# Two sets of GELU buffers in the low-rank FFN of a two-block transformer layer

## The reference

```
x = x + attn_a(layernorm(x))   # causal attention with low-rank q and kv, rope, 16 heads, scores clipped to +-80
x = x + ffn(layernorm(x))
x = x + attn_b(layernorm(x))   # causal attention in a window of 256, 16 heads
x = x + ffn(layernorm(x))

def ffn(x):                    # U1 1024x256, V1 256x4096, U2 4096x256, V2 256x1024
    P = x @ U1
    H = gelu(P @ V1 + b1)      # the tanh form of gelu
    Q = H @ U2
    return Q @ V2 + b2
```

## Time and profile before

| | |
|---|---|
| median of 3 runs | 16249.39 us (16242.38 to 16249.87) |
| the profiled execution, its own time | 16244.88 us |
| its span, slowest core (core 1) | 16243.3 us |
| spans of the 8 cores | 16207.3 to 16243.3 us |
| mean granted TensorE clock of the cores | 0.536 to 0.540 of full speed |
| busy on core 1 | PE 5935.0, PE weight loads 4271.9, DVE 5274.7, ACT 4021.9, POOL 118.0 us |

### The profile page before, as it was taken

How to read it: one execution, slowest core, us unless ns; L and a number is a source line. 1 busy time by engine, 2 the same in 40 slices (tenths; PEclk the granted TensorE clock), 3 DMA queues, 4 the chain that set the end, 5 groups by cost and what they waited for, 6 DMA issues and landing times.

```text
span 16243.3 us, 153437 instructions; the slowest of 8 cores (16207.3 to 16243.3 us)
## 1 busy us (share of the span) xinstructions
PE 5935.0 (37%) x54352; PEld 4271.9 (26%) x54352; DVE 5274.7 (32%) x7648; ACT 4021.9 (25%) x9384; POOL 118.0 (1%) x228
## 2 busy tenths in 40 slices
PE   2333322333333344344443333333333333333333
PEld 1111112222233233333343222222222222222222
DVE  0111134444444444444444322232233222232233
ACT  2222222222222222222232222222222222222222
POOL 0000000000000000000000000000000000000000
PEclk6555555555555555555555555555555555555555
DMA  1111011111122122222232200000000000000000
GB/s 64 37 37 37 31 32 33 35 38 45 51 58 63 48 62 70 54 79 60 72 81 54 83 19 6 6 6 6 6 6 6 3 6 6 6 6 6 6 6 4
DMA packets 197816, 540.34 MB, mean 33 GB/s; under 512 B 33876, under 2 KB 34261, under 8 KB 192600
## 3 DMA queue, kind: packets, MB, share of 16 engines
q1 hardware_dynamic: 177112, 463.40, 10.7%
q0 software_dynamic: 19968, 67.12, 1.0%
HBM read 463.29 MB, written 67.11 MB: 33 GB/s over the span
## 4 chain that ended last, share of the span: by engine, by line
DVE 29%; PE 29%; ACT 25%; issue 10%; DMA 5%; ACTq 1%; SPq 1%; DVEq 1%; POOL 0%; POOLq 0%
DVE bufA L342 11%; PE pf L649 7%; ACT ptb L557 7%; DVE pbig L551 4%; ACT hb L322 4%; PE pbig L542 3%; PE pbig L350 2%; PE acc L579 2%; DVE htb L344 2%; DVE bufA L333 2%; ACT bufA L326 2%; ACT bufB L336 2%; DMA arena<-vS 2%; PE pbf L284 2%; ACT xnT L288 2%
## 5 line engine op out<-in xcount | busy, mean ns | idle before, releaser
L551 DVE TENSOR_SCALAR pbig<-pbig 128x1024 f32<-128x1024 f32 x1056 | 1251.6, 1227 | 2016.6 <-PE pbig L542 2016.6
L342 DVE RECIPROCAL bufA<-bufB 128x512 f32<-128x512 f32 x512 | 1716.7, 3353 | 53.6 <-DVE bufB L339 0.9
L312 PE MATMUL pbig<-ptf,W_v 128*128 128x128 bf16 x4096 | 518.0, 306 | 3303.7 <-ACT bufB L336 3264.8
L557 ACT ACTIVATE ptb<-pbig 128x1024 bf16<-128x1024 f32 x1056 | 1081.1, 1024 | 2383.2 <-DVE pbig L551 2331.6
L579 PE MATMUL acc<-arena,ptb 128*128 128x64 bf16 x8448 | 815.0, 215 | 1336.3 <-ACT ptb L557 1109.6
L312 PEld LDWEIGHTS pbig<-ptf,W_v 128*128 128x128 bf16 x4096 | 396.4, 138 | 3425.3 <-issue 3425.3
L649 PE MATMUL pf<-xnT,arena 128*64 128x128 bf16 x8192 | 1055.2, 309 | 615.1 <-ACT qTs L656 309.3
L542 PE MATMUL pbig<-arena 96*128 96x128 bf16 x8448 | 986.0, 311 | 446.7 <-DMA arena<-vS 440.1
L322 ACT ACTIVATE hb<-pbig,sb_b1r 128x128 f32<-128x128 f32 x2048 | 584.4, 368 | 2272.5 <-DVE htb L344 2188.8
L579 PEld LDWEIGHTS acc<-arena,ptb 128*128 128x128 bf16 x8448 | 705.0, 126 | 1504.2 <-issue 1504.2
L649 PEld LDWEIGHTS pf<-xnT,arena 128*64 128x64 bf16 x8192 | 838.5, 166 | 830.2 <-issue 830.2
(11 more groups left out here) (108 smaller groups left out, 7154.8 us busy)
## 6 DMA issues: line engine op xcount, KB each, us to landing
arena<-kcS SPq DMA_DIRECT2D x528, 256.0 KB, 3.5
arena<-vS SPq DMA_DIRECT2D x528, 256.0 KB, 3.5
arena<-krS SPq DMA_DIRECT2D x528, 128.0 KB, 3.8
xa<-x SPq DMA_DIRECT2D x64, 512.0 KB, 5.3
x2S<-x2sb POOLq DMA_DIRECT2D x32, 512.0 KB, 4.6
xa<-x2S SPq DMA_DIRECT2D x32, 512.0 KB, 3.8
out<-x2sb POOLq DMA_DIRECT2D x32, 512.0 KB, 4.5
rc<-ropec SPq DMA_DIRECT2D x32, 256.0 KB, 4.9
```

The costliest lines, as they stand in the source:

```text
L312: emit("tensor", lambda e, j=j, l=l, pb=pb, jj=jj: e.matmul(pbig[:, pb + jj * 128:pb + (jj + 1) * 128], wb["v1"][:, l * 4096 + j * 128:l * ...
L342: emit("vector", lambda e: e.reciprocal(out=sg[:], in_=dd[:]), incs=[("v", 1)])
L551: emit("vector", lambda e, h0=h0: e.tensor_scalar(out=pbig[:, h0 * 128:(h0 + 8) * 128], in0=pbig[:, h0 * 128:(h0 + 8) * 128], scalar1=80.0 ...
L557: emit("scalar", lambda e, kb=kb, h0=h0: e.activation(out=ptb[kb][:, h0 * 128:(h0 + 8) * 128], in_=pbig[:, h0 * 128:(h0 + 8) * 128], func= ...
```

## The change

The work tiles of the GELU chain now exist twice. Even groups use `hb0`, `bufA`, `bufB`; odd groups use `hb1`, `bufC`, `bufD`. The rope tables `rc` and `rs` lose their own memory and lie in `bufC` and `bufD`. The waits of the loop name a count in place of "everything so far": TensorE waits, ahead of L312 of group g, for the bias additions of group g-2 (which read the same PSUM region), and ScalarE waits, ahead of L322, for L344 of group g-2 (the last reader of the same work tiles). Ahead of the square ScalarE is given the same wait once more. Group 0 has in addition the wait of TensorE for all of ScalarE's work. The order of the instructions in every queue stays as it was, and so do their number, shapes and types. No DMA is added, removed or moved.

```diff
-        rc = [T("rc0", [128, 512])]
-        rs = [T("rs0", [128, 512])]
...
-        hb = T("hb", [128, 512])
+        hbb = [T("hb0", [128, 512]), T("hb1", [128, 512])]
         bufA = T("bufA", [128, 512])
         bufB = T("bufB", [128, 512])
+        bufC = T("bufC", [128, 512])
+        bufD = T("bufD", [128, 512])
...
+        rc = [bufC]
+        rs = [bufD]
...
+                idmark = {0: 0, 1: 0}
+                htmark = {0: 0, 1: 0}
                 for g in range(8):
                     pb = 1024 + (g % 2) * 512
-                    wait("tensor", "s")
+                    hb = hbb[g % 2]
+                    A_ = bufA if g % 2 == 0 else bufC
+                    B_ = bufB if g % 2 == 0 else bufD
+                    wait("tensor", "s", idmark[g % 2])
+                    if g == 0:
+                        wait("tensor", "s")
...
                     wait("scalar", "t")
-                    wait("scalar", "v")
+                    wait("scalar", "v", htmark[g % 2])
...
+                    idmark[g % 2] = cnt["s"]
                     wait("scalar", "s")
-                    emit("scalar", lambda e: e.activation(out=sq[:], in_=hb[:], func=AF.Square),
+                    wait("scalar", "v", htmark[g % 2])
+                    emit("scalar", lambda e, hb=hb, A_=A_: e.activation(out=A_[:], in_=hb[:], func=AF.Square),
                          incs=[("s", 1)])
...
-                    emit("vector", lambda e, g=g: e.tensor_tensor(out=htb[:, g * 512:(g + 1) * 512],
-                                                                  in0=hb[:], in1=sg[:], op=ALU.mult),
+                    emit("vector", lambda e, g=g, hb=hb, A_=A_: e.tensor_tensor(out=htb[:, g * 512:(g + 1) * 512],
+                                                                                in0=hb[:], in1=A_[:], op=ALU.mult),
                          incs=[("v", 1)])
+                    htmark[g % 2] = cnt["v"]
```

More of the change, by code:

```diff
@@ L318, in ffn @@
                     wait("scalar", "t")
-                    wait("scalar", "v")
+                    wait("scalar", "v", htmark[g % 2])
                     for jj in range(4):
                         j = g * 4 + jj
-                        emit("scalar", lambda e, j=j, jj=jj, pb=pb: e.activation(
+                        emit("scalar", lambda e, j=j, jj=jj, pb=pb, hb=hb: e.activation(
                             out=hb[:, jj * 128:(jj + 1) * 128], in_=pbig[:, pb + jj * 128:pb + (jj + 1) * 128],
@@ L324, in ffn @@
                             func=AF.Identity, bias=b1r[:, j:j + 1]), incs=[("s", 1)])
+                    idmark[g % 2] = cnt["s"]
                     wait("scalar", "s")
-                    emit("scalar", lambda e: e.activation(out=sq[:], in_=hb[:], func=AF.Square),
+                    wait("scalar", "v", htmark[g % 2])
+                    emit("scalar", lambda e, hb=hb, A_=A_: e.activation(out=A_[:], in_=hb[:], func=AF.Square),
                          incs=[("s", 1)])
                     wait("vector", "s")
-                    emit("vector", lambda e: e.tensor_scalar(out=u0[:], in0=sq[:], scalar1=GC2,
-                                                             scalar2=GC1, op0=ALU.mult, op1=ALU.add),
+                    emit("vector", lambda e, A_=A_, B_=B_: e.tensor_scalar(out=B_[:], in0=A_[:], scalar1=GC2,
+                                                                           scalar2=GC1, op0=ALU.mult, op1=ALU.add),
@@ L331, in ffn @@
                          incs=[("v", 1)])
                     wait("vector", "v")
-                    emit("vector", lambda e: e.tensor_tensor(out=uu[:], in0=u0[:], in1=hb[:], op=ALU.mult),
+                    emit("vector", lambda e, hb=hb, A_=A_, B_=B_: e.tensor_tensor(out=A_[:], in0=B_[:], in1=hb[:], op=ALU.mult),
                          incs=[("v", 1)])
                     wait("scalar", "v")
-                    emit("scalar", lambda e: e.activation(out=ee[:], in_=uu[:], func=AF.Exp, scale=-2.0),
+                    emit("scalar", lambda e, A_=A_, B_=B_: e.activation(out=B_[:], in_=A_[:], func=AF.Exp, scale=-2.0),
@@ L337, in ffn @@
                          incs=[("s", 1)])
                     wait("vector", "s")
-                    emit("vector", lambda e: e.tensor_scalar_add(out=dd[:], in0=ee[:], scalar1=1.0),
+                    emit("vector", lambda e, B_=B_: e.tensor_scalar_add(out=B_[:], in0=B_[:], scalar1=1.0),
                          incs=[("v", 1)])
                     wait("vector", "v")
-                    emit("vector", lambda e: e.reciprocal(out=sg[:], in_=dd[:]), incs=[("v", 1)])
+                    emit("vector", lambda e, A_=A_, B_=B_: e.reciprocal(out=A_[:], in_=B_[:]), incs=[("v", 1)])
```

## The result

The changed kernel takes 15199.56 us (median of 8 runs, 15193.92 to 15204.0), beside 16245.64 us for the kernel before in the same comparison: a ratio of 0.9356 with a 95% interval of 0.9346 to 0.9366. It is faster by 1046 us. The prediction was 15290 us with a range of 15230 to 15400. Those 90 us are what the experiments are about.

A forecast was written before the change was run, and what follows sets the result against it. The prediction took a relay between engines, not a full engine, to bound the kernel. 448 x 2.14 = 959 us off 16244.88 gave 15286, plus 4.5 for the median, so 15290 us; other terms were 0; range 15230 to 15400.

The forecast's parts named there:

- The relay and its passages: GELU loop, L344 to L329 of the next group: 2.75 us becomes 0.61, saving 2.14 us in each of 448 passages.
- rival 1: L344 to L329: VectorE needs 0.80 us instead of 0.61, as for dependent pairs; 15376 us, chance 0.08.
- rival 2: L322 and L326 under L342: ScalarE and VectorE don't run together in SBUF; saving 0.37 us a passage, 16084 us, chance 0.04.
- rival 4: Loop waits: a count still covers L344 of group g-1 or another wait blocks; old relay, 16249 us, chance 0.02.
- rival 5: Reciprocal L342: stretched by ScalarE's traffic, making the kernel slower; 16791 us if it doubled, chance 0.02.
- TensorE's wait: Ahead of L312: its matmuls move forward by more than a group, but nothing waits for them; 0 us.
- the tiles of the rope tables: `rc` and `rs` in `bufC` and `bufD`: used in phase 1 alone, with a barrier between; 0 us.
- the second wait: Ahead of the square L326: same count as ahead of L322, hence already met; 0 us.
- the instant of the rise: TensorE's clock rising within L350 behind the loop: put near 0, far ends 178 us lost or 205 us gained.
- no distance moves: Outside the loop: a sign expected in the profile after, that no distance there changes.
- rival 3: Clock behind the loop, at L350, moves: 15468 or 15085 us at the ends, chance 0.06 for both sides together.
- L350 clearly away from 6.4 us: L350's 64 matmuls: a total clearly different from 6.4 us would be the sign of rival 3.

The follow-up runs named there:

- the two kernels with Q in the loop: Kernel before and changed kernel, each with the 8 matmuls of Q that need group g run inside the loop: 15976.93 and 14961.81 us.

## Why the prediction was right, and where it was wrong

**The relay and its passages: right.** 448 passages at 2.14 us were to give 959 us; the loop gave 968. The start of L341 0.61 us behind L356, the group of 6.64 us (6.65 expected), ScalarE's idle time of 4.2 us ahead of the exponential (about 4.0 expected) and the 766 us left ahead of L329 (some 780 expected) came as written, but for L332, which starts 0.09 us before the exponential's end and not behind it. Of the 9 us more, about half is the passage shown, 8.79 - 6.64 = 2.15 us and not 2.14; the other half lies in passages that had run longer than the one shown: before, a loop took 4335.2 / 64 = 67.74 us, 0.17 more than 6.04 + 7 x 8.79; after, 52.61, 0.10 more than 6.03 + 7 x 6.64.

**Rivals 1, 2, 4 and 5: fell.** The trace gives 0.61 us and not 0.80, the reciprocal 3352 to 3354 ns with ScalarE at work under it, and L332 is not released by the group before any more. With the Trainium skill's statement (SBUF — State Buffer, "Who interferes with whom") that ScalarE and VectorE have their own ports the trace agrees: 3353 ns alone, 3353 and 3352 ns together.

**TensorE's wait, the tiles of the rope tables, the second wait: right at 0.** The run with TensorE's wait alone is at a ratio of 1.0000, and the run without it (0.9359) is level with the changed kernel.

**The step that failed: "What may move is the instant of the rise ... The row of the start at 0.50 after a rest puts it near 0."** The start at 0.50 was right and said nothing about the rise. In phase 3 the rise stood 5.36 us after the start of L350 and moved to 3.12, and the term that was set to 0 measured 52 us at L350. Another 24 us came in phase 3 outside the function, in the projections of V and of the output, where the prediction had written that no distance moves. With the 52 us alone put back the time would be 15251 us, inside the range. The prediction had rival 3 for this with a gain of up to 205 us and a chance of 0.06, and the range's lower end took in only 60 us of it; by its own sign, L350 clearly away from 6.4 us (5.52 in the call shown), rival 3 is in part what happened. Its error was to reason from a rest's effect on TensorE, a thing that the runs with a rest of 10.4 us in place of 22.7 and of 24.2 in place of 12.6 show to be without influence here, instead of asking how the loop's new length would place L350 against the rise. Four kernels with added work show that the instant matters and does not move along with the start of L350: 1.06 us ahead of L350 cost 0.01 or 3.07 us a tile, depending on where the rise stood.

The Trainium skill's warning (TensorE: Matmul & The Clock Gate, "HAM oscillation — how this bites in real kernels") that gaps throttle TensorE holds for the start of L350, which is at 0.50 in every call of every trace here in which the 64 matmuls stand behind the loop. As a warning against this change it did not come true.

**What stays open.** What fixes the instant of the rise is not shown; the runs show only that it shifts against L350 when the time ahead of L350 changes, and less or otherwise when the same time is added behind it. Whether it can be foretold for a new length of the loop is untested: no run changed that length in small steps. Of the 36 us between the two kernels with Q in the loop, 5 are not placed. The 23 to 26 us of phase 1 that some kernels save in the landing of x stay open too.

## What to carry to other kernels

In a relay between engines, count the passages and read one of them: what a second set of buffers brings is the time from the late instruction to the early one, less the start-to-start time of two independent neighbours, as long as the engine taken off the path has time to spare (2.8 us here); a trace holds all three. Where a run of matmuls starts at the low clock and the clock rises within it, treat its length as uncertain by the distance between all low and all high, and expect an edit elsewhere in a periodic loop to move it either way. Before crediting a small edit with tens of us, add a known delay and see whether it costs its own length.

## What the runs showed of the hardware that was not expected

A program's repeated part can hold its length against added work. With 1.06 us added to each tile ahead of L350, phase 3 of the kernel before stayed at 214.25 us a tile (214.24 without): the 64 matmuls spent more of their time at 2.4 GHz and gave back 0.57 us a tile, and the two projections, which the added work does not touch, gave back another 0.43. From the fifth tile on the median tile took 215.04, 215.06 and 215.12 us with 0, 1.06 and 2.12 us added in the kernel before, and 197.96, 201.32 and 201.38 us in the changed one; so the length stands still against some of the added work and then takes more than all of it at once. The shortened loop of the changed kernel, 15.13 us a call less, took 214.24 - 197.32 = 16.92 us off a tile in the same way.
